# Decay in two waves, key norms in decay's bank, values masked from SBUF, another order on SyncE, and a last inverse on two engines

## The chip, the cores and the metric

The kernel runs on one core of a Trainium2 chip. The metric is the device time of one execution in microseconds (us). The median of the three runs of the kernel before is 1072.9 us.

## The reference

The input is x, 8 sequences of 512 tokens with 256 channels in float32. An attention-like layer with a recurrent state is followed by a mixture of eight experts. Cut to what matters here:

```python
xx = shift(x) - x;  lo = tanh((x + xx*maa_x) @ maa_w1.T) -> 4 x 32 -> @ maa_w2
xrg, xwa, xk, xv = x + xx*(lo + time_maa)
r, k, v = xrg @ Wr.T, xk @ Wk.T, xv @ Wv.T;   g = tanh(xrg @ gate_w1.T) @ gate_w2
w  = -softplus(-(time_decay + tanh(xwa @ decay_w1.T) @ decay_w2)) - 0.5
kk = k + tanh(xk @ kkk_w1.T) @ kkk_w2;  kk = kk / max(norm of each head(kk), 1e-12)
a, ma, mk = sigmoid(...)                       # three more low-rank products
k  = (k*ma + k*a*(1-ma)) * exp(w*mk);  b = -kk*a;  wt = exp(-exp(w))
for t in range(512):                           # state s: 16 x 16 for each head
    s = s*wt[t] + (s @ kk[t]) b[t]^T + v[t] k[t]^T;   y[t] = s @ r[t]
x1 = layernorm(x + ((groupnorm(y) + bonus*v) * g) @ Wo.T)
e  = argmax(x1 @ centroids.T)                  # one expert for each token
out = layernorm(x1 + ffn_e(layernorm(x1)))     # 256 -> 1024 -> 256, relu
```

## The kernel before

The 512 time steps are cut into 16 blocks of 32 steps (NBLK = 16, `last` = 15). Within a block the recurrence is solved with the inverse of a triangular 32x32 matrix for each of the 128 pairs of head and sequence, one pair in each partition. Every engine runs `body(n)` for n from -2 to 18, written out by hand. Body n computes the projections, decays, keys and scores of block n+1, turns keys and values of block n, solves and reads out block n-1, normalizes and projects block n-2, and routes block n-3. So several blocks are in flight, and each engine's order within a body is the order of the code. After the bodies, 39 blocks of 128 tokens go through the experts.

What sets the order around the change:

- **PSUM banks.** Six banks are handed from job to job. A job such as `z@1` (the decay's product in bank 1) may start when the job before it in that bank has been emptied, as the table `freed` says. PE waits for that with `wait_empty`.
- **TensorE (PE).** In `body`: `hidden`, `gates`, `square k`, `turn_keys`, then `decay_a_kk` and `ma_mk` (line 622), the router's `logit` and the projection `wo` of older blocks, `solve`, `norms`, the squares r and v, the read-outs, `scores` (line 662), `update`, and the next block's `low_1` and `low_2` (line 594). `fill` (line 576) is a helper that many of these use. All is float32, and each matmul leaves two records in the trace.
- **ScalarE (ACT).** `keep_k` (line 1085) copies k to SBUF; then come z plus its bias (line 1029, `halves`), its sigmoid, a, ma, |z|, the squares of kk, mk, a table load, the logarithm of sigma (line 1117), and much later `keep_v` and `mask_v`.
- **VectorE (DVE).** A body begins where `xm_stage` (lines 1389, 1392) of g=1 reads `low_2`. Then follow `normed`, the other xm stages, `keep_r`, `gated` (line 1536, which frees the bank of g for ma), `difference`, `mix_stage`, `sum_kk` (line 1420), `sum_decays`, `key_gain`, `add_tokens` (1546), `gain_keys`, `token_stats` (1552 to 1556), `key_exponent` (1412, which needs the logarithm), `keep_x` (1511), and the keys and removals down to `mask_keys` (1445), after which PE may start `scores`.
- **GpSimd (POOL).** It inverts one block per body with 60 small operations (lines 1911 and 1914), behind a memset of the diagonal (line 1904) that waits for the scores to come back from DRAM.
- **SyncE (SP).** One DMA queue: scores out (478), scores back as one matrix per partition (483), the inverse out (491), tokens for `add_tokens` (460), the inverse back by heads (502), tokens after the layer norm out (468), and the expert weights W2 (513), of which four are loaded in body 15 and four in body 16.

## Time and profile before

| | |
|---|---|
| runs | 1076.72, 1072.90, 1069.43 us; median 1072.9 |
| profiled execution | 1076.19 us, of which the span is 1074.1 us |
| mean granted TensorE clock | 0.951 |
| busy: PE / PE weight load | 980.1 us (91%) / 801.8 us (75%) |
| busy: DVE / ACT / POOL | 768.0 (71%) / 519.9 (48%) / 613.1 us (57%) |

Times in the rows are microseconds from the start of the span. The first 52 us are a start-up, the 15 repeated bodies run up to about 670 us, then comes a stretch of some 80 us with the last block and the routing, and from about 760 us the experts, in which PE is busy nearly all the time. "Busy" for PE counts modelled ends of pipelined matmuls.

### The profile page before, as it was taken

The page shows a single profiled execution, that of the slowest core. Times are in us where ns is not written, and L with a number is a line of the kernel's source. Part 1 is how long each engine was busy: PE and PEld are TensorE (multiplying, and loading weights), DVE is VectorE, ACT ScalarE, POOL GpSimd, SP SyncE. Part 2 cuts the span into 40 slices and gives each one's busy share as a digit, 9 for nine tenths or more (in the row PEclk, how much of TensorE's full clock was granted, in tenths as well). Part 3 has the DMA queues.
Part 4 walks back from the last instruction along what each step waited for, and adds up shares of the span by engine and source line. Part 5 has one row for each costly group of instructions (what it writes and reads, how often), then busy time and mean ns, then how long its engine had stood idle before and what let it go on. Part 6 is the DMA issues. An engine that isn't in the chain of part 4 may idle for free.

```text
span 1074.1 us, 42156 instructions
## 1 busy us (share of the span) xinstructions
PE 980.1 (91%) x16652; PEld 801.8 (75%) x16653; DVE 768.0 (71%) x1793; ACT 519.9 (48%) x1081; POOL 613.1 (57%) x1135
## 2 busy tenths in 40 slices
PE   8898989999999989999999998679899999999995
PEld 5676777777777767777777776557899898989894
DVE  5766788889879778887688885266476666666663
ACT  4474576677677576676476783221122121212120
POOL 1088786788886787785867876810133333333321
PEclk9997999999999999998799998689999999999998
DMA  5113225225324225224143133746545445544430
GB/s 121 40 21 81 71 33 110 65 51 111 77 47 101 70 44 111 72 42 107 17 101 87 28 91 85 206 115 232 217 163 176 161 174 162 176 158 170 158 119 4
DMA packets 208894, 112.14 MB, mean 104 GB/s; under 512 B 172508, under 2 KB 192224, under 8 KB 208352
## 3 DMA queue, kind: packets, MB, share of 16 engines
q1 hardware_dynamic: 202352, 100.92, 35.0%
q0 software_dynamic: 3744, 8.40, 2.3%
q8 instruction: 121, 1.98, 0.8%
q10 hardware_dynamic: 2640, 0.54, 0.3%
q14 instruction: 37, 0.30, 0.1%
HBM read 85.57 MB, written 26.08 MB: 104 GB/s over the span
## 4 chain that ended last, share of the span: by engine, by line
PE 61%; DVE 14%; issue 8%; POOL 6%; DMA 5%; ACT 4%; DVEq 1%; SPq 1%; ACTq 0%; POOLq 0%
PE bank L576 16%; PE bank L970 12%; PE bank L983 9%; PE bank L662 6%; PE ry L983 4%; PE bank L718 3%; POOL arena L1914 3%; POOL arena L1911 3%; DVE bank L1389 2%; PE ry L692 2%; PE bank L594 1%; PE bank L622 1%; PE bank L950 1%; PE ry L698 1%; PE bank L740 1%
## 5 line engine op out<-in xcount | busy, mean ns | idle before, releaser
L576 PE MATMUL bank<-arena 128*128 128x256 f32 (+2 forms) x992 | 280.9, 422 | 22.4 <-DVE arena L1434 9.5
L1914 POOL TENSOR_TENSOR arena<-arena 128x30 f32<-128x30 f32 (+14 forms) x480 | 261.6, 545 | 37.6
L1911 POOL TENSOR_TENSOR arena<-arena 128x30 f32<-128x30 f32 (+14 forms) x480 | 250.5, 522 | 36.4
L576 PEld LDWEIGHTS bank<-arena 128*128 128x128 f32 x992 | 178.5, 203 | 67.9 <-issue 31.5
L970 PEld LDWEIGHTS bank<-arena 128*128 128x128 f32 x1248 | 146.8, 194 | 5.8 <-issue 3.0
L970 PE MATMUL bank<-arena 128*128 128x128 f32 x1248 | 147.5, 277 | 3.1 <-DVE arena L1820 2.5
L1498 DVE TENSOR_TENSOR arena<-bank,arena 128x512 f32<-128x512 f32 x128 | 79.5, 684 | 53.1 <-PE bank L662 53.1
L1302 ACT ACTIVATE arena<-arena 128x1 f32<-128x1 f32 x39 | 11.5, 294 | 178.6 <-DVE arena L1774 178.6
L983 PE MATMUL bank<-arena 128*128 x416 | 96.4, 385 | 0.1
L1945 POOL COPY arena<-arena 128x1 int32 (+1 forms) x39 | 7.1, 183 | 146.4 <-DVE arena L1838 146.4
L983 PEld LDWEIGHTS bank<-arena 128*128 128x128 f32 x416 | 76.9, 190 | 14.5 <-issue 4.9
L662 PE MATMUL bank<-arena 32*128 32x64 f32 x2048 | 68.9, 276 | 10.6 <-issue 6.4
L1939 POOL DMA_INDIRECT arena<-scr_x,arena x39 | 41.2, 1056 | 62.4 <-DVE arena L1756 31.4
L662 PEld LDWEIGHTS bank<-arena 32*128 32x128 f32 x2048 | 64.0, 189 | 14.9 <-issue 13.4
L1389 DVE SCALAR_TENSOR_TENSOR bank<-bank,arena 128x256 f32<-128x256 f32 x128 | 56.1, 484 | 22.2 <-PE bank L594 22.2
L670 PE MATMUL bank<-arena 128*128 128x128 f32 x432 | 62.5, 279 | 4.2 <-DVE arena L1511 1.6
L670 PEld LDWEIGHTS bank<-arena 128*128 128x128 f32 x432 | 52.1, 144 | 18.8 <-issue 12.4
L1904 POOL MEMSET arena<- 128x32 f32 x16 | 2.5, 157 | 111.2 <-DMA arena<-scr_n 111.2
L718 PEld LDWEIGHTS bank<-arena 32*64 32x64 f32 x2048 | 40.1, 157 | 34.6 <-issue 29.6
L1820 DVE TENSOR_SCALAR arena<-bank,arena 128x128 f32<-128x128 f32 x156 | 43.9, 345 | 24.6 <-issue 19.9
L1947 POOL DMA_INDIRECT out_dram<-arena x39 | 39.8, 1021 | 34.9 <-DVE arena L1804 20.8
L718 PE MATMUL bank<-arena 32*64 32x32 f32 x2048 | 43.8, 239 | 15.1 <-DMA arena<-scr_u 13.9
(173 smaller groups left out, 1757.7 us busy)
## 6 DMA issues: line engine op xcount, KB each, us to landing
arena<-in_W SPq DMA_DIRECT2D x47, 1024.0 KB, 5.1
scr_n<-arena SPq DMA_DIRECT2D x64, 128.0 KB, 3.0
arena<-scr_n SPq DMA_DIRECT2D x16, 512.0 KB, 3.7
scr_u<-arena SPq DMA_DIRECT2D x16, 512.0 KB, 4.5
arena<-scr_u SPq DMA_DIRECT2D x62, 128.0 KB, 2.9
arena<-in_xTp SPq DMA_DIRECT2D x32, 132.0 KB, 4.0
arena<-in_x SPq DMA_DIRECT2D x64, 64.0 KB, 2.7
scr_x<-arena SPq DMA_DIRECT2D x64, 64.0 KB, 1.8
```

What stands on the lines that cost most here:

```text
L576: mm = pe.matmul(ring.tile(m, name)[0:rows, to], lhsT, rhs, start=(i == 0), stop=(i == len(terms) - 1))
L662: mm = pe.matmul(ring.tile(m, f"sc{f}{p}")[:, b * 2 * TB:(b + 1) * 2 * TB], bkm[r, f * B + b, :], aq[m % 2][r, f * B + b].rearrange("p x t ...
L670: mm = pe.transpose(ring.tile(m, name)[:, i * P:(i + 1) * P], src, ident)
L718: mm[bank] = pe.matmul(ring.tile(m, f"x{bank}")[x_rows_of(e), at:at + 32], Ux[m % 2][r, g % 4, g // 4, e].rearrange("p h t -> p (h t)"), R ...
L970: mm = pe.matmul(hidT_ps[t // 4][:, (t % 4) * P:(t % 4 + 1) * P], W1[s][:, k, t * P:(t + 1) * P], xnT[:, k, :], start=(k == 0), stop=(k == ...
L983: mm = pe.matmul(y_ps[s][:, 0:D], hidT[s][:, t, :], W2f[:, bass.ds(e * (FT * D) + t * D, D)], start=(t == 0), stop=(t == FT - 1))
L1389: xm_ok.inc(m, f"{g}{h}", STT(out=part, in0=part, scalar=prm(f"maa{g}", h), in1=dx[:, h], op0=ALU.add, op1=ALU.mult))
L1498: score.inc(m, name, TT(sc[m % 2][:, f, p].rearrange("p k e x t -> p (k e) (x t)"), ring.tile(m, name)[:, :].rearrange("p (b n) -> p b n", ...
L1820: relu_dve.inc(str(t), nc.vector.tensor_scalar(hidT[s][:, t], hidT_ps[1][:, (t - 4) * P:(t - 3) * P], b1f[:, bass.ds(e * FT + t, 1)], 0.0, ...
L1911: inv_ok.inc(f"m{s}", TT(t, U[:, 0:s, s:s + 1].broadcast_to(shape), U[:, s:s + 1, s + 1:TB].broadcast_to(shape), ALU.mult))
L1914: inv_ok.inc(f"a{s}", TT(U[:, 0:s, s + 1:TB], U[:, 0:s, s + 1:TB], t, ALU.add))
L1939: nc.gpsimd.indirect_dma_start(out=xg[:, s], out_offset=None, in_=x_rows, in_offset=bass.IndirectOffsetOnAxis(ap=index, axis=0), bounds_ch ...
```

## The change

The parts, as the code has them:

1. **Two waves.** The decay's product z was one matmul per half of the channels over all 128 rows (two slots), followed by two slots with a and kk side by side and two with ma and mk. Now z is cut into two products over 32 rows each. A first wave (two slots) runs the first z part, a and kk side by side in three row groups; a second wave runs the second z part, ma and mk. z is full only after the second.
2. **kk in k's bank.** The low-rank part of kk is added by PE into the bank where k stands, so it must wait until ACT has kept k. `sum_kk` on DVE is gone; ACT gets `keep_kk`, a copy of 128x512, and squares from PSUM. k moves ahead of the gates on PE.
3. **Banks.** `ss` goes to bank 1, `logit` to bank 0 ahead of `wo` in the same bank, `xa` to 5, `bk11` and `v0` to 0. The matmuls for `ss`, `yc` and `var` are two of 256 columns rather than one of 512.
4. **ACT order.** a before z; kk and its square, then the logits, before ma; `mask_v` reads SBUF and stands behind the second `keep_values`; `key_decay` and `growths` ahead of `keep_keys(1,1)`.
5. **DVE order.** `token_stats` moves behind `keep_decay`, `decay_reads` behind `bonus_terms`.
6. **SyncE.** Tokens are loaded behind the heads of the inverse; the inverse of block 14 is stored ahead of the scores' load of block 15; W2 is loaded in body 16 only.
7. **The last inverse.** POOL does the left 24 columns; DVE does the right 8 columns in bank 2, in three pieces among its other work of body 15.

```diff
@@ -356,7 +364,7 @@
         freed = {"lo1": [(low_act, "lo1")], "h": [(hid_act, "decay"), (hid_act, "copy"), (hid_act, "kkk")],
                  "z": [(comb, "scan")],
                  "a": [(proj, "a1")], "ma": [(comb, "k2")], "mk": [(comb, "e2")], "tg": [(proj, "tg")], "k": [(proj, "k")],
-                 "r": [(comb, "rk"), (comb, "q")], "v": [(proj, "v"), (proj, "vm1")], "kk": [(comb, "kk")], "ss": [(comb, "bm1")],
+                 "r": [(comb, "rk"), (comb, "q")], "v": [(proj, "v")], "kk": [(proj, "sq")], "ss": [(comb, "bm1")],
                  "rk": [(comb, "u")], "su": [(state_dve, "s")],
                  "yc": [(post_act, "c1"), (post_act, "s")], "var": [(post_dve, "w")], "g": [(post_dve, "g1")], "wo": [(tok, "z")],
                  "xT": [(late_act, "x1T")], "logit": [(late_act, "lg")]}
@@ -367,9 +375,9 @@
         freed["xa"] = [(chain_dve, "xae"), (chain_dve, "xao")]
         freed["xb"] = [(chain_act, "xb0"), (chain_act, "xb1"), (chain_dve, "xbo")]
         filled = [sem(f"filled{i}") for i in range(len(banks))]
-        ring = Ring(banks, [(0, "bk00@5"), (1, "h@2"), (-2, "g@4"), (1, "k@3"), (0, "bk01@2"), (1, "z@1 a@5 kk@3 ma@4 mk@2"),
-                            (-3, "logit@3"), (-2, "wo@0"), (1, "ss@0"), (-1, "xa@1 xb@3"), (1, "r@4"),
-                            (0, "bk11@5"), (1, "v@2"), (0, "bk10@5 v0@1 v1@3"),
+        ring = Ring(banks, [(0, "bk00@5"), (1, "h@2"), (1, "k@3"), (-2, "g@4"), (0, "bk01@2"), (1, "a@5 kk@3"),
+                            (1, "z@1 ma@4 mk@2"), (-3, "logit@0"), (-2, "wo@0"), (1, "ss@1"), (-1, "xa@5 xb@3"), (1, "r@4"),
+                            (0, "bk11@0"), (1, "v@2"), (0, "bk10@5 v0@0 v1@3"),
                             (1, "rk@4"), (-1, "su@0"), (1, "sc00@2 sc01@5 sc02@3 sc03@1 tg@4"), (2, "lo1@5"),
                             (1, "sc10@2 sc11@5 sc12@1 sc13@4"), (-1, "yc@3"), (2, "lo2_1@2 lo2_2@5 lo2_0@0 lo2_3@1"),
                             (-1, "var@4"), (-2, "xT@3")], filled, freed)
...
+                if m == last:
+                    store_inverse(last - 1)
                 sp.wait_ge(n_out, (m + 1) * 64)
                 if m >= 2:
                     sp.wait_ge(u_out, (m - 1) * 16)
                 sp.dma_start(Up[m % 2].rearrange("p r c -> p (r c)"),
                              nd.rearrange("g k f e (h s) t -> (g k f e h) (s t)", h=2)).then_inc(n_in, 16)
-
-            def inverse_to_heads(m):
-
-                inv_ok.wait(sp, m, "a1")
+                if m == last:
+                    heads_from_inverse(last - 1)
+
+            def store_inverse(m):
...
                 sp.dma_start(ud, Up[m % 2].rearrange("p r c -> p (r c)")).then_inc(u_out, 16)
-                if m == last:
-                    load_tokens(last)
-                elif m and m - 1 < last - 1:
-                    load_tokens(m - 1)
+
+            def heads_from_inverse(m):
+
...
                 for p in range(PAIRS if m < last else 2):
                     sp.dma_start(heads_of(m, p), u_rows[p]).then_inc(u_in, 16)
+                if m == last:
+                    load_tokens(last)
+                elif m and m - 1 < last - 1:
+                    load_tokens(m - 1)
...
             def body(n):
-                if has(n - 1):
-                    inverse_to_heads(n - 1)
+                if has(n - 1) and n != last:
+                    store_inverse(n - 1)
+                    heads_from_inverse(n - 1)
                 if has(n - 3) and n <= last:
                     store_x1(n - 3)
-                if n == last:
+                if n == last + 1:
+                    sp.wait_ge(u_in, NBLK * 64)
                     load_experts(slice(0, 4))
-                if n == last + 1:
                     load_experts(slice(4, E))
...
+                    ring.wait_empty(pe, m, name)
+                for h, to in both:
+                    mm_z = pe.matmul(ring.tile(m, "z")[:, to], w_out[0:32, 2, hs(h)], hid[0:32, :], start=(h == 0), stop=False,
+                                     skip_group_check=True)
+                    mm_a = pe.matmul(ring.tile(m, "a")[:, to], w_out[64:96, 0, hs(h)], hid[64:96, :], start=True, stop=True)
+                    mm_kk = pe.matmul(ring.tile(m, "kk")[:, to], w_out[96:128, 0, hs(h)], kkh[96:128, :], start=False, stop=True,
+                                      skip_group_check=True)
+                mm_z.then_inc(half_decay, 1)
+                ring.fill(m, "a", mm_a)
+                ring.fill(m, "kk", mm_kk)
+
+            def decay_ma_mk(m):
+                pe.wait_ge(half_decay, m + 1)
+                for name in ("ma", "mk"):
+                    ring.wait_empty(pe, m, name)
+                for h, to in both:
+                    mm_z = pe.matmul(ring.tile(m, "z")[:, to], w_out[32:64, 2, hs(h)], hid[32:64, :], start=False, stop=True,
+                                     skip_group_check=True)
+                    mm_ma = pe.matmul(ring.tile(m, "ma")[:, to], w_out[64:96, 1, hs(h)], hid[64:96, :], start=True, stop=True)
+                    mm_mk = pe.matmul(ring.tile(m, "mk")[:, to], w_out[96:128, 1, hs(h)], hid[96:128, :], start=True, stop=True)
+                ring.fill(m, "z", mm_z)
+                ring.fill(m, "ma", mm_ma)
+                ring.fill(m, "mk", mm_mk)
 
             def square(m, name, w, x):
                 weights(m)
                 xm_ok.wait(pe, m, f"x{x}")
-                fill(m, name, [(to, [(w_sq[:, w, k, hs(h)], xm[x][:, k]) for k in range(HALF)]) for h, to in both])
+                fill(m, name, [(to, [(w_sq[:, w, k, hs(h)], xm[x][:, k]) for k in range(HALF)]) for h, to in both],
+                     started_once=(name == "k"))
 
...
+                proj.inc(m, "sq", A(flat(nrm), bank(m, "kk"), ACT.Square))
+
+            def keep_kk(m):
+                if m:
+                    comb.wait(act, m - 1, "kkn")
+                ring.wait_full(act, m, "kk")
+                proj.inc(m, "kk", A(flat(kk), bank(m, "kk"), ACT.Copy))
...
+                proj.wait(act, m, "v")
                 for h in range(2):
-                    proj.inc(m, f"vm{h}", A(vm[:, :, h], bank(m, "v").rearrange("p (g t) -> p g t", t=TB), ACT.Copy,
-                                            scale=odd_even[:, h:h + 1]))
+                    proj.inc(m, f"vm{h}", A(vm[:, :, h], tt(vt), ACT.Copy, scale=odd_even[:, h:h + 1]))
...
+            def keep_coefs(m):
+                act.wait_ge(n_in, (m + 1) * 16)
+                last_inv.wait(act, 0, "diag")
+                comb.wait(act, m, "e2")
+                A(coefs, Up[m % 2][:, 0:CUT, 0:CUT], ACT.Copy).then_inc(coefs_kept, 1)
...
                 if has(n + 1):
+                    keep_a(n + 1)
                     keep_z(n + 1)
                     sigma_of_z(n + 1)
-                    keep_a(n + 1)
+                    keep_kk(n + 1)
+                    square_kk(n + 1)
+                if has(n - 3):
+                    keep_logits(n - 3)
+                if has(n + 1):
                     keep_ma(n + 1)
                     abs_of_z(n + 1)
-                if has(n - 3):
-                    keep_logits(n - 3)
                 if n == last + 1:
                     second_inverse_to_heads(last)
                 if has(n + 1):
-                    square_kk(n + 1)
                     sigma_of_abs(n + 1)
                     keep_mk(n + 1)
...
+                if has(n + 1):
+                    key_decay(n + 1)
+                    growths(n + 1)
                 if has(n) and n < last:
                     keep_keys(n, 1, 1)
...
                 if has(n + 1):
                     keep_v(n + 1)
-                    mask_v(n + 1)
                 if has(n):
                     keep_values(n, 1)
+                if has(n + 1):
+                    mask_v(n + 1)
...
+            def start_right(m):
+                dve.wait_ge(n_in, (m + 1) * 16)
+                last_inv.wait(dve, 0, "diag")
+                last_inv_dve.inc("start", nc.vector.tensor_copy(right, Up[m % 2][:, :, CUT:TB]))
+                dve.wait_ge(coefs_kept, 1)
+                proj.wait(dve, m, "iW0", "iW1")
+
+            def invert_right(m, steps):
+                U = Up[m % 2]
+                for s in steps:
+                    last_inv_dve.wait(dve, 0, "start" if s == TB - 2 else f"a{s + 1}")
+                    c = max(s + 1, CUT) - CUT
+                    n = TB - CUT - c
+                    shape = [P, s, n]
+                    t = flat(L)[:, 0:s * n].rearrange("p (r c) -> p r c", r=s)
+                    column = U[:, 0:s, s:s + 1] if s >= CUT else coefs[:, 0:s, s:s + 1]
+                    last_inv_dve.inc(f"m{s}", TT(t, right[:, s:s + 1, c:].broadcast_to(shape), column.broadcast_to(shape), ALU.mult))
+                    last_inv_dve.wait(dve, 0, f"m{s}")
+                    last_inv_dve.inc(f"a{s}", TT(right[:, 0:s, c:], right[:, 0:s, c:], t, ALU.add))
+
+            def keep_right(m):
+                last_inv_dve.wait(dve, 0, "a1")
+                last_inv_dve.inc("kept", nc.vector.tensor_copy(Up[m % 2][:, :, CUT:TB], right))
...
-                if has(n - 2):
+                if has(n - 2) and not has(n + 1):
                     token_stats(n - 2)
                 if has(n + 1):
                     key_exponent(n + 1)
+                if n == last:
+                    start_right(last)
+                    invert_right(last, range(TB - 2, 23, -1))
                 if has(n - 1):
                     keep_x(n - 1, "a", 0)
                     keep_x(n - 1, "a", 1)
                     keep_x(n - 1, "b", 1)
+                if n == last:
+                    invert_right(last, range(23, 12, -1))
                 if has(n + 1):
                     normed_kk(n + 1)
-                    decay_reads(n + 1)
                     decay_kk(n + 1)
                     removal(n + 1)
                     decay_keys(n + 1)
                     bonus_terms(n + 1)
+                    decay_reads(n + 1)
                 if has(n + 1):
                     mask_removal(n + 1)
                     mask_keys(n + 1)
                     bonus_values(n + 1)
                     keep_decay(n + 1)
+                if has(n - 2) and has(n + 1):
...
+            def invert_left(m):
+
+                pool.wait_ge(n_in, (m + 1) * 16)
+                U = Up[m % 2]
+                inv_ok.wait(pool, m - 1, "a1")
+                last_inv.inc("diag", nc.gpsimd.memset(U.rearrange("p r c -> p (r c)")[:, 0:TB * TB:TB + 1], 1.0))
+                pool.wait_ge(coefs_kept, 1)
+                for s in range(CUT - 2, 0, -1):
+                    n = CUT - 1 - s
+                    shape = [P, s, n]
+                    t = Ut[:, 0:s * n].rearrange("p (r c) -> p r c", r=s)
+                    if s < CUT - 2:
+                        last_inv.wait(pool, 0, f"a{s + 1}")
+                    last_inv.inc(f"m{s}", TT(t, U[:, 0:s, s:s + 1].broadcast_to(shape), U[:, s:s + 1, s + 1:CUT].broadcast_to(shape),
+                                             ALU.mult))
+                    last_inv.wait(pool, 0, f"m{s}")
+                    last_inv.inc(f"a{s}", TT(U[:, 0:s, s + 1:CUT], U[:, 0:s, s + 1:CUT], t, ALU.add))
+
+            for m in range(NBLK - 1):
                 invert(m)
+            invert_left(last)
```

PE, in the middle of the program, from `hidden` of one block to the `wo` of an older one (bank0 to bank5 are the six banks; L610/L631 is `hidden`, L670/L698 `turn_keys`). Before:

```order
L610 MATMUL bank2<-arena 32x256 x8
L576 MATMUL bank4<-arena 128x256 x2
L576 MATMUL bank3<-arena 128x256 x4
L670 MATMUL bank2<-arena 128x128 x4
L622 MATMUL bank1<-arena 128x256 x2
L622 MATMUL bank5<-arena 128x256
L622 MATMUL bank3<-arena 128x256
...
L576 MATMUL bank3<-arena 128x8 x4
L576 MATMUL bank0<-arena 128x256 x4
```

and now:

```order
L631 MATMUL bank2<-arena 32x256 x8
L596 MATMUL bank3<-arena 128x256 x4
L596 MATMUL bank4<-arena 128x256 x2
L698 MATMUL bank2<-arena 128x128 x4
L640 MATMUL bank1<-arena 128x256
L642 MATMUL bank5<-arena 128x256
L643 MATMUL bank3<-arena 128x256
...
L654 MATMUL bank1<-arena 128x256
L656 MATMUL bank4<-arena 128x256
...
L596 MATMUL bank0<-arena 128x8 x4
L596 MATMUL bank0<-arena 128x256 x4
```

z (bank1) was complete two matmuls after `turn_keys`; now its last matmul stands in the second wave, beside ma's in bank4, and logit (128x8) and wo share bank0.

ACT at the same place, from `keep_k` to the logarithm. Before:

```order
L1085 ACTIVATE arena<-bank3 128x512
L1150 ACTIVATE arena<-bank2 128x512
L1029 ACTIVATE arena<-bank1,arena 128x256 x2
L1058 ACTIVATE bank1<-arena 128x512
L1029 ACTIVATE arena<-bank5,arena 128x256 x2
L1029 ACTIVATE bank4<-bank4,arena 128x256 x2
L1064 ACTIVATE arena<-arena 128x512
L1212 ACTIVATE arena<-bank3 128x16
L1097 ACTIVATE arena<-arena 128x512
L1068 ACTIVATE arena<-arena 128x512
L1029 ACTIVATE bank2<-bank2,arena 128x256 x2
L1035 ACT_TABLE_LOAD
```

and now:

```order
L1182 ACTIVATE arena<-bank2 128x512
L1057 ACTIVATE arena<-bank5,arena 128x256 x2
L1057 ACTIVATE arena<-bank1,arena 128x256 x2
L1086 ACTIVATE bank1<-arena 128x512
L1130 ACTIVATE arena<-bank3 128x512
L1124 ACTIVATE arena<-bank3 128x512
L1244 ACTIVATE arena<-bank0 128x16
L1057 ACTIVATE bank4<-bank4,arena 128x256 x2
L1092 ACTIVATE arena<-arena 128x512
L1096 ACTIVATE arena<-arena 128x512
L1057 ACTIVATE bank2<-bank2,arena 128x256 x2
L1063 ACT_TABLE_LOAD
```

a (bank5) went ahead of z (bank1), the copy of kk from bank3 (L1130) is new, and the logits (128x16) are read two operations later.

SyncE's queue in one body, from the scores' load. Before:

```order
L483 DMA arena<-scr_n 128x1024 [waits u_out,n_out]
L491 DMA scr_u<-arena 128x1024 [waits u_in,inv_ok]
L460 DMA arena<-in_x 32x2x256 [waits x1_out,filled3]
L460 DMA arena<-in_x 32x2x256 x3
L502 DMA arena<-scr_u 32x32x32 [waits filled3,u_out]
L502 DMA arena<-scr_u 32x32x32 x3
```

and now:

```order
L493 DMA arena<-scr_n 128x1024 [waits u_out,n_out]
L507 DMA scr_u<-arena 128x1024 [waits u_in,inv_ok]
L517 DMA arena<-scr_u 32x32x32 [waits filled3,u_out]
L517 DMA arena<-scr_u 32x32x32 x3
L468 DMA arena<-in_x 32x2x256 [waits x1_out,filled3]
L468 DMA arena<-in_x 32x2x256 x3
```

The four token loads (in_x) went from ahead of the four loads of heads to behind them.

## Rows read from the trace of the kernel before

**Rows 1.** Busy time by stretch: PE, PEld, DVE, ACT, POOL, granted clock, DMA share, GB/s.

```profile
257.20:298.30 41.10, 38.08 (x921) 29.62 (x917) 35.64 (x64) 29.94 (x59) 35.48 (x68) 1.00 0.43 90
380.40:421.40 41.00, 37.43 (x905) 29.04 (x904) 32.87 (x61) 26.82 (x50) 33.04 (x63) 0.96 0.34 75
```

**Rows 2.** Timeline, DVE, one body: start, us, operation, [idle before, releaser].

```profile
326.85 0.88 DVE L1389 SCALAR_TENSOR_TENSOR bank<-bank,arena 128x256 f32<-128x256 f32 x2 [0.70 <-PE bank L594]
...
334.95 0.83 DVE L1536 SCALAR_TENSOR_TENSOR arena<-arena,bank 128x256 f32<-128x256 f32 x2
...
337.41 0.68 DVE L1420 TENSOR_TENSOR arena<-bank,arena 128x512 f32<-128x512 f32 x1
...
341.20 0.69 DVE L1546 TENSOR_TENSOR arena<-bank,arena 128x512 f32<-128x512 f32 x1 [0.67 <-PE bank L576]
...
342.40 0.75 DVE L1552 BATCH_NORM_STATS2 arena<-arena 128x6 f32<-128x256 f32 x2
...
343.35 0.93 DVE L1412 SCALAR_TENSOR_TENSOR arena<-arena 128x512 f32<-128x512 f32 x1
...
352.13 1.75 DVE L1445 TENSOR_TENSOR arena<-arena 128x512 f32<-128x512 f32 x2
```

**Rows 3.** Timeline, ACT, the same body.

```profile
334.41 0.60 ACT L1085 ACTIVATE arena<-bank 128x512 f32<-128x512 f32 x1 [0.95 <-PE bank L576]
...
335.72 0.84 ACT L1029 ACTIVATE arena<-bank,arena 128x256 f32<-128x256 f32 x2 [0.22 <-PE bank L622]
...
337.12 0.82 ACT L1029 ACTIVATE arena<-bank,arena 128x256 f32<-128x256 f32 x2
...
342.53 0.63 ACT L1117 ACTIVATE arena<-arena 128x512 f32<-128x512 f32 x1
```

**Rows 4.** Timeline, PE, the same body.

```profile
325.59 1.15 PE L594 MATMUL bank<-arena 32*128 32x256 f32 x16
...
334.59 2.96 PE L622 MATMUL bank<-arena 128*128 128x256 f32 x20
338.23 2.86 PE L576 MATMUL bank<-arena 128*128 128x8 f32 x16 [0.69 <-DVE arena L1420]
...
342.08 1.13 PE L576 MATMUL bank<-arena 128*128 128x512 f32 x2
...
346.47 1.89 PE L576 MATMUL bank<-arena 128*128 128x256 f32 x8
```

**Rows 5.** Timeline, DVE, another body: its first operation and its key_exponent.

```profile
450.69 0.88 DVE L1389 SCALAR_TENSOR_TENSOR bank<-bank,arena 128x256 f32<-128x256 f32 x2 [2.00 <-PE bank L594]
...
468.76 1.05 DVE L1412 SCALAR_TENSOR_TENSOR arena<-arena 128x512 f32<-128x512 f32 x1
```

**Rows 6.** Timeline, SP's queue, the body of rows 2; then issues, 300 to 400 us, median landing.

```profile
331.50 2.64 SPq L460 DMA_DIRECT2D arena<-in_x  x4
335.18 2.67 SPq L502 DMA_DIRECT2D arena<-scr_u  x4
...
arena<-in_x SPq DMA_DIRECT2D x8, 64.0 KB, 2.9
```

**Rows 7.** One line, L1904: durations in ns, first and last start in us.

```profile
L1904 POOL MEMSET arena<- x16: 154/158/162, 52.2 to 668.0; 128x32 f32 x16
```

**Rows 8.** The chain that ended last, around the last solve.

```profile
702.91 2.76 DMA scr_u<-arena
...
710.15 1.97 PE bank L718 x64
```

**Rows 9.** Timeline, DVE, 655 to 765 us: last tokens' wait, and small operations.

```profile
670.96 0.69 DVE L1546 TENSOR_TENSOR arena<-bank,arena 128x512 f32<-128x512 f32 x1 [6.11 <-DMA arena<-in_x]
...
703.67 0.39 DVE L1579 TENSOR_TENSOR arena<-arena 128x224 f32<-128x224 f32 x1
...
738.73 0.77 DVE L1710 TENSOR_TENSOR arena<-bank,arena 128x8 f32<-128x8 f32 x4 [0.72 <-PE bank L930]
```

**Rows 10.** Timeline, POOL, an inverse operation of 130 elements.

```profile
656.71 0.44 POOL L1914 TENSOR_TENSOR arena<-arena 128x130 f32<-128x130 f32 x1
```

## What the change should do to the time

> **What bounds the kernel now.** I read the table of stretches first. In the repeated bodies PE is busy 37.4 to 38.1 us of 41, DVE 33 to 36, POOL 33 to 35, ACT 27 to 30 [rows 1], so no engine is the bound by its share alone. The bodies have a mean length of (668.0 - 52.2) / 15 = 41.05 us [rows 7]. Which wait ends last is read from one body, engine by engine.
>
> DVE starts the body at 326.85, when PE's `low_2` is there, and works without a gap to 337.41, idles 0.67 us at `add_tokens`, and goes on to the end of `mask_keys` at 353.88 [rows 2]. Only then may PE start `scores`. So from the start of a body to `mask_keys`, 27.0 us, DVE is the chain; from there to the next body's start PE is. PE waits for DVE in the first part too: 0.69 us for `sum_kk`, which empties bank 3 for the router's logits [rows 4].
>
> One point inside DVE's stretch is tied to ACT. `key_exponent` starts at 343.35 [rows 2] and needs the logarithm that ACT finishes at 342.53 + 0.63 = 343.16 [rows 3]. In the timeline ACT works back to back from 335.72, the start of z, to that logarithm: 7.44 us. So DVE may be made shorter ahead of `key_exponent` as one likes: it then waits for ACT.
>
> **The bodies, term by term.**
>
> PE's saving. The group of L622 is six slots of 256 columns in 2.96 us [rows 4], 0.49 each. In L594 eight matmuls in four row groups take 1.15 us for two slots [rows 4], so three side by side should cost one slot. Six slots become four: 0.98 us less. One matmul of 512 columns takes 1.13 us, four of 256 take 1.89 [rows 4], so two of 256 take 0.95: 0.18 less, or by the start of the next group 0.12. I take 0.15, three times. PE has 1.4 us less to do in each body.
>
> DVE's saving. `sum_kk` 0.68 us goes, and `token_stats`, 343.35 - 342.40 = 0.95 us, moves behind `keep_decay`, where DVE waits for `scores` anyway [rows 2]. 1.6 us less ahead of `key_exponent`. `decay_reads` only changes places ahead of `mask_keys`; it is worth nothing there.
>
> What z now waits for. Wave 2 writes ma in bank 4, which `gated` empties at 334.95 + 0.83 = 335.78 [rows 2]. Two slots later, at 335.8 + 1.0 = 336.8, z is full. Before, z was full after the first two slots, 334.59 + 0.98 = 335.57 [rows 4], and ACT started on it at 335.72 [rows 3]. ACT's z therefore starts at about 336.95, 1.2 us later. It does a (0.82 us [rows 3]) in the meantime and still idles 0.35. Then z to the logarithm takes 7.44 - 0.82 (a is done) + 0.60 (the copy `keep_kk`, priced as the copy `keep_k` [rows 3]) = 7.2 us, so the logarithm is ready at 344.2 and `key_exponent` starts at about 344.3 instead of 343.35: 0.95 us later. DVE would have been there at 341.7. All of DVE's 1.6 us is idle time, and what lies behind `key_exponent` is unchanged up to `mask_keys`.
>
> In PE's order the projection `wo` now shares bank 0 with the logits, which ACT reads at about 339.6. PE idles near 1.8 us before it; its `wo` is full near 341.7, where `add_tokens` could start 0.5 us after its place of now. That is hidden by the wait for ACT.
>
> So a body like this one becomes 0.95 us longer up to `mask_keys`. From there to the next start only the halved `yc` counts: 0.15 less. Together +0.8.
>
> Not every body is like this. From a body's start to `key_exponent` it is 16.5 us here [rows 2] and 18.07 in another [rows 5]; the same two operations give 16.1 to 16.8 in eight of the 13 full bodies and 17.9 to 18.6 in five, where PE's slower `wo` held DVE up. In those five the ACT chain (17.45) is shorter than what there is, and PE's saving gives back 0.2 to 0.4. The mean over the 13 is (8 x 0.85 - 5 x 0.3) / 13 = +0.4, less 0.15 for `yc`: about +0.3 us for each body, **+4 us** in all. Bounds: -1.35 for each body if ACT is not in the way (rival A), +1 if every body is like the first.
>
> By the Trainium skill, page "TensorEngine Tiling (Array Packing)", section "PSUM Bottleneck", tiling speeds up TensorE but not the emptying of PSUM, and the copies may become the bottleneck. By PE's slots alone the body would be 1.4 us shorter; by the page's rule, which here is the ACT chain above, it is longer.
>
> **Masks, values, banks.** `mask_v` out of SBUF costs the same on ACT and moves behind `keep_values`. Nothing waits for it before the next body. I put nothing on it. `ss` in two halves falls in PE's slack.
>
> **SyncE.** Token loads are issued at 331.50 and the heads at 335.18, when the stored inverse has landed [rows 6]. The heads are held by that landing, not by the token loads, so they gain nothing. The tokens now follow: the last is issued near 337.85 + 2.0 and lands 2.9 later [rows 6], at 342.8; `add_tokens` and `gain_keys` are then over at 344.1, just ahead of the new `key_exponent`. Zero in this body, with no room left.
>
> **The last inverse.** POOL starts the last one at 668.0 [rows 7] and its result is stored at 702.91 [rows 8]: 34.9 us. Nothing of the next blocks covers it; `solve` starts 7.24 us behind the store [rows 8]. POOL's left part has 44 operations of at most 132 elements, 0.44 us each [rows 10] and some 0.06 between them: under 22 us, over before 691. DVE's right part decides. An operation of 8 elements follows the one before it in 0.20 us (four in 0.77), one of 224 takes 0.39 [rows 9]; that is 0.19 + 0.9 ns for each element. The 60 operations have 2 x 2936 elements: 11.4 + 5.3 = 16.7 us, two copies 0.8, some gaps: 19. It starts behind `add_tokens` and its statistics for block 13, which waited for tokens until 670.96 [rows 9]. In the new queue the inverse of block 14 is stored about 5.7 us earlier, but the tokens stand behind its heads: they land near 672, the statistics end at 674, and DVE's part starts there. `keep_x` 2.0, `next_state` 1.4 and `tokens` 0.9 lie between its pieces. 674 + 19 + 4.3 = 697.5, against 702.9: **-5 us**. The rest behind it runs as before, W2's load included: it is 8 MB from body 16 on, needed only some 60 us later. Bounds: -7 (tokens land early), 0 (strided operands on DVE cost 1.3 times as much).
>
> **Sum.** 1076.2 (the profiled execution, 1074.1 of span and 2.1 around it) + 4 - 5 = 1075. That execution is 3.3 us above the median of the three runs, so against the median: **1072 us**, no change that can be measured. About 1% is what a measurement of this kernel can tell from none.
>
> **The rivals.**
>
> A, faster: PE sets the period after all, and ACT keeps up, because its operations overlap more than I allow or because `gated` comes earlier. Then each of 14 bodies gives back PE's 1.35 us: -19, with the inverse -24: 1049 us. For it: PE is busy over 91% of a body [rows 1]. Against it: ACT has no gap between z and the logarithm. Chance 0.34.
>
> B, slower: the granted clock. One stretch ran at 1.00, another at 0.96 [rows 1]; 0.04 of 41 us is 1.6 us of PE time given up, at 1.2 instead of 2.4 GHz for some 3.3 us. In the change PE has less to do and new idle places, 1.8 us ahead of `wo` and about 1 us ahead of `scores`. If every body loses those 1.6 us where about half do now, that is +0.8 x 14 = 11, with all bodies at +0.8 for ACT another 11, less 5: 1090 us. It decides once the mean granted clock of the bodies falls under about 0.95. Chance 0.16.
>
> The Trainium skill, "TensorE: Matmul & The Clock Gate", section "What's actually happening", says that the slow clock is the default and activity releases it. The difference between the two stretches fits that; by it, the less PE has to do, the more often B.
>
> C, slower: tokens too late. In bodies where the stored inverse lands 1 to 2 us later than in [rows 6], `add_tokens` holds DVE for as long. +0.7 x 14 = 10: 1082 us. For it: there is no room left even in the body shown. Chance 0.08.
>
> The forecast has 0.42. The range leaves out a tenth on each side: 1048 to 1088; the forecast's own is 1064 to 1081. Faster by over 1%: 0.34. Within 1%: 0.42. Slower: 0.24.
>
> **What would show it.** Right: DVE waits 1 us or more before `key_exponent` and names ACT; its start is 17.3 to 17.6 us behind the body's start; the mean length of a body, from one diagonal memset to the next, stays 41 to 41.6 us; the last inverse takes 29 to 30 us from its memset to its store. Wrong: bodies under 40 us with PE busy near 37 (A); a mean clock under 0.94 (B); `add_tokens` waiting for `in_x` in most bodies (C); DVE's operations for the right part at 0.4 us each, which would leave the last inverse no shorter.

## The result, and the profile after

| | before | changed |
|---|---|---|
| median | 1071.2 us (4 runs) | 1117.4 us (4 runs) |
| ratio to before | | 1.0425, 95% interval 1.0364 to 1.0487 |
| span of the profiled execution | 1074.1 us | 1117.0 us |
| mean granted clock | 0.951 | 0.922 |
| first diagonal memset | 52.2 us | 54.7 us |
| last diagonal memset | 668.0 us | 708.6 us |
| from one to the next | 41.05 us | 43.60 us |
| last memset to the first gather of the experts | 82.4 us | 82.7 us |
| the experts to the end | 323.6 us | 325.6 us |

Medians are over all executions of a kernel; the ratios leave out the few that ran in a slower state. The change made the kernel 4.25% slower, 46 us. The forecast was 1072 us, at the top 1088. Of the 42.9 us between the two spans, 2.5 are there before the first memset, 15 x 2.54 = 38.1 in the bodies, 0.3 between the last memset and the experts, and 2.0 in the experts. The bodies are the case. The profiled execution of the kernel before took 1076.19 us, 5 above its median, that of the changed kernel 1118.81, 1.4 above, so 2.54 us for each body is rather too little than too much.

The memset that opens each inverse answers to [rows 7]. In the changed kernel the last one has a line of its own. The trace, by source line: durations in ns, first and last start in us.

```profile
L1974 POOL MEMSET arena<- x15: 154/157/162, 54.7 to 664.0; 128x32 f32 x15
L1991 POOL MEMSET arena<- x1: 156/156/156, 708.6 to 708.6; 128x32 f32 x1
```

The page of the changed kernel: busy time, the granted clock in 40 slices, and the costliest group of instructions.

```profile
span 1117.0 us, 42510 instructions
PE 1001.3 (90%) x16812; PEld 833.6 (75%) x16813; DVE 776.4 (70%) x1839; ACT 536.0 (48%) x1098; POOL 597.5 (53%) x1119
PEclk9997998899989999788799997888999999999998
L596 PE MATMUL bank<-arena 128*128 128x256 f32 (+1 forms) x1088 | 310.6, 430 | 41.0 <-ACT arena L1244 22.5
```

What is new in the last line is what ends TensorE's idle time: the same line before reads 22.4 us idle and names VectorE. L1244 is ScalarE's copy of the router's logits, and TensorE idles 22.5 us in all for it. The waits of TensorE and VectorE in the bodies (230 to 650 us; us in total, times, longest) say how often:

```profile
PE bank L596 <- ACT arena L1244: 17.8, 10, 1.8
...
DVE arena L1443 <- ACT bank L1086: 13.3, 10, 1.6
DVE arena L1549 <- PE bank L746: 12.6, 7, 3.1
...
DVE arena L1608 <- DMA arena<-in_x: 2.0, 1, 2.0
```

1.8 us in each of ten bodies, ahead of `wo`. What comes behind it is to be seen in the timeline of TensorE in one of them (line 596 is `fill`, 746 `solve`, 698 `turn`; each matmul leaves two records, so x8 are four matmuls):

```profile
317.23 1.06 PE L596 MATMUL bank<-arena 128*128 128x8 f32 x8
320.07 2.77 PE L596 MATMUL bank<-arena 128*128 128x256 f32 x8 [1.78 <-ACT arena L1244]
322.76 1.93 PE L746 MATMUL bank<-arena 32*64 32x32 f32 x64
324.63 2.08 PE L596 MATMUL bank<-arena 128*128 128x256 f32 x4
326.63 1.93 PE L746 MATMUL bank<-arena 32*64 32x32 f32 x64
328.49 3.37 PE L596 MATMUL bank<-arena 128*128 128x256 f32 x8
331.70 0.60 PE L698 MATMUL bank<-arena 128*128 128x128 f32 x4
332.14 1.89 PE L596 MATMUL bank<-arena 128*128 128x256 f32 x8
```

Four matmuls of 256 columns take 3.37 us at 328.49, and the next four, at 332.14, take 1.89 as in [rows 4]. The rows of the stretches (columns as in [rows 1]) give the granted clock:

```profile
320.10:321.00 0.90, 0.90 (x4) 0.80 (x5) 0.33 (x2) 0.90 (x3) 0.74 (x3) 1.00 0.64 184
321.10:331.30 10.20, 10.20 (x144) 7.88 (x143) 6.27 (x10) 7.71 (x14) 9.10 (x15) 0.50 0.27 50
332.00:333.00 1.00, 1.00 (x7) 0.91 (x6) 0.90 (x3) 0.60 (x1) 0.85 (x2) 1.00 0.00 0
```

The clock is at full speed in the first microsecond of `wo`, then at half for 10.2 us in which TensorE is busy without a gap. From `wo` to the end of the square r it is 331.86 - 320.07 = 11.8 us; in a kernel below, where nothing runs slowly, 7.1. On VectorE, in the same body, it arrives as the wait of `keep_x` (line 1549) for the solve:

```profile
307.13 0.88 DVE L1432 SCALAR_TENSOR_TENSOR bank<-bank,arena 128x256 f32<-128x256 f32 x2 [0.69 <-PE bank L615]
...
318.95 1.22 DVE L1443 TENSOR_TENSOR_SCAN arena<-arena,bank 128x512 f32<-128x512 f32 x1 [1.19 <-ACT bank L1086]
320.74 0.69 DVE L1449 SCALAR_TENSOR_TENSOR arena<-bank,arena 128x512 f32<-128x512 f32 x1 [0.57 <-ACT bank L1057]
...
324.51 0.69 DVE L1455 SCALAR_TENSOR_TENSOR arena<-arena 128x512 f32<-128x512 f32 x1 [0.28 <-ACT arena L1149]
...
328.61 2.01 DVE L1549 TENSOR_TENSOR arena<-bank,arena 64x512 f32<-64x512 f32 x3 [2.69 <-PE bank L746]
...
335.95 1.75 DVE L1483 TENSOR_TENSOR arena<-arena 128x512 f32<-128x512 f32 x2
```

`key_exponent` (1455) starts 17.38 us behind the body's start, as forecast. But `keep_x` (1549) then waits 2.69 us for a solve at half speed, and from `key_exponent` to `mask_keys` (1483) it is 11.44 us. In [rows 2] that is 8.78, and `keep_x` does not wait.

### The profile page after: what moved, and what is told of

The parts are those of the page before. It is cut to its first block, busy times and chain, and to the rows that moved or that the text cites. A ratio compares the mean times of both kernels' runs of the same rounds, so it can differ in the third digit from the quotient of the medians.

```text
span 1117.0 us, 42510 instructions
## 1 busy us (share of the span) xinstructions
PE 1001.3 (90%) x16812; PEld 833.6 (75%) x16813; DVE 776.4 (70%) x1839; ACT 536.0 (48%) x1098; POOL 597.5 (53%) x1119
## 4 chain that ended last, share of the span: by engine, by line
PE 65%; DVE 15%; issue 8%; ACT 6%; DVEq 2%; DMA 2%; SPq 1%; POOL 0%; ACTq 0%; POOLq 0%
PE bank L596 20%; PE bank L1011 9%; PE bank L998 6%; PE bank L690 6%; PE bank L746 3%; PE bank L698 3%; PE ry L720 2%; PE ry L726 2%; PE bank L615 2%; PE bank L768 1%; PE bank L654 1%; PE bank L631 1%; DVEq L1830 1%; PE ry L1011 1%; PE ry L821 1%
## 5 line engine op out<-in xcount | busy, mean ns | idle before, releaser
L596 PE MATMUL bank<-arena 128*128 128x256 f32 (+1 forms) x1088 | 310.6, 430 | 41.0 <-ACT arena L1244 22.5
L596 PEld LDWEIGHTS bank<-arena 128*128 128x128 f32 x1088 | 217.5, 220 | 95.3 <-issue 50.3
L1984 POOL TENSOR_TENSOR arena<-arena 128x30 f32<-128x30 f32 (+14 forms) x450 | 244.0, 542 | 35.3
L1981 POOL TENSOR_TENSOR arena<-arena 128x30 f32<-128x30 f32 (+14 forms) x450 | 236.5, 526 | 34.1
L998 PEld LDWEIGHTS bank<-arena 128*128 128x128 f32 x1248 | 146.8, 194 | 6.1 <-issue 3.3
L1011 PEld LDWEIGHTS bank<-arena 128*128 128x128 f32 x416 | 76.9, 190 | 14.5 <-issue 4.9
L698 PE MATMUL bank<-arena 128*128 128x128 f32 x432 | 63.1, 279 | 9.2 <-DVE arena L1549 6.3
L698 PEld LDWEIGHTS bank<-arena 128*128 128x128 f32 x432 | 51.7, 143 | 19.4 <-issue 10.6
L746 PEld LDWEIGHTS bank<-arena 32*64 32x64 f32 x2048 | 43.8, 171 | 20.8 <-issue 14.2
L2036 POOL DMA_INDIRECT out_dram<-arena x39 | 39.8, 1021 | 34.9 <-DVE arena L1874 20.8
L1360 ACT ACTIVATE arena<-bank,arena 128x128 f32<-128x128 f32 x156 | 44.6, 369 | 26.4 <-PE bank L998 26.4
```

The costliest lines, as they stand in the source:

```text
L596: mm = pe.matmul(ring.tile(m, name)[0:rows, to], lhsT, rhs, start=(i == 0 and not (started_once and j)), stop=(i == len(terms) - 1), skip_ ...
L698: mm = pe.transpose(ring.tile(m, name)[:, i * P:(i + 1) * P], src, ident)
L746: mm[bank] = pe.matmul(ring.tile(m, f"x{bank}")[x_rows_of(e), at:at + 32], Ux[m % 2][r, g % 4, g // 4, e].rearrange("p h t -> p (h t)"), R ...
L998: mm = pe.matmul(hidT_ps[t // 4][:, (t % 4) * P:(t % 4 + 1) * P], W1[s][:, k, t * P:(t + 1) * P], xnT[:, k, :], start=(k == 0), stop=(k == ...
L1011: mm = pe.matmul(y_ps[s][:, 0:D], hidT[s][:, t, :], W2f[:, bass.ds(e * (FT * D) + t * D, D)], start=(t == 0), stop=(t == FT - 1))
L1360: relu_act.inc(str(t), A(hidT[s][:, t], hidT_ps[0][:, t * P:(t + 1) * P], ACT.Relu, bias=b1f[:, bass.ds(e * FT + t, 1)]))
```

## The experiments

All kernels were timed beside runs of the kernel before on the same chip; each ratio is to those, with its 95% interval. "Body" is the mean from one diagonal memset to the next in one profiled execution, worked out as in the table above; two executions of a kernel can differ in it by 0.5 us and more (those of the kernel before that the ratios use took 1063 to 1080 us, which is 1.1 us for each body), so small differences are read from the ratios. "Clock" is the granted clock from 93 to 639 us of that execution. "Idle" is TensorE's wait for the logits ahead of `wo`, in one body; the kernel before waits 0.7 us elsewhere, for `sum_kk` [rows 4]. An unread matmul has 256 columns and takes some 0.5 us.

| kernel | idle | clock | body | ratio |
|---|---|---|---|---|
| before | none | 0.96 | 41.05 | 1 |
| changed | 1.8 | 0.89 | 43.60 | 1.0425 [1.0364, 1.0487] |
| changed, one unread matmul | 1.3 | 0.95 | 42.04 | 1.0255 [1.0147, 1.0363] |
| changed, logits before kk | 0.8 | 0.96 | 41.35 | 1.0217 [1.0119, 1.0316] |
| changed, three unread matmuls | 0.4 | 0.97 | 41.26 | 1.0142 [1.0066, 1.0218] |
| changed, early logits | none | 0.97 | 41.99 | 1.0242 [1.0150, 1.0335] |
| changed, z first | 0.6 | 0.95 | 41.41 | 1.0045 [0.9991, 1.0100] |
| before, shared bank | 0.9 | 0.92 | 42.02 | 1.0184 [1.0100, 1.0267] |
| before, shared bank, two unread matmuls | none | 0.97 | 40.51 | 1.0027 [0.9993, 1.0060] |
| before, waves | none | 0.93 | 41.80 | 1.0135 [1.0044, 1.0227] |

### The wait itself, or the clock behind it

Three matmuls that nobody reads fill most of the wait; the wait for ScalarE's copy stays.

```diff
+                if has(n - 3) and n < last:
+                    ring.wait_empty(pe, n - 1, "xa")
+                    keep_busy(3, banks[5])
                 if has(n - 2):
                     project_out(n - 2)
```

> The changed kernel with three matmuls of 256 columns, whose result nobody reads, put on TensorE between the logits and `wo` in bodies 3 to 14 (bank 5, which is free there). They take about 1.4 of the 1.8 us that TensorE idles; the wait for ScalarE's copy of the logits stays where it is, `wo` starts when it did. It tells the wait itself from the clock that falls behind it. If the clock is what costs (theory T in its clock form): `wo` takes 1.9 us instead of 2.8, the solve 1.13 us instead of 1.93, the bodies come down by 1.5 to 2 us, about 1090 to 1095 us. If the wait itself costs: 1115 to 1118 us, with bodies of 43.5 us at a higher clock.

Measured: 1086.3 us, under the 1090 to 1095 expected. The timeline of TensorE at the same place of a body (line 821 is `keep_busy`; each matmul leaves two records):

```profile
348.80 1.06 PE L596 MATMUL bank<-arena 128*128 128x8 f32 x8
349.72 1.54 PE L821 MATMUL bank<-arena 128*128 128x256 f32 x6
351.65 1.97 PE L596 MATMUL bank<-arena 128*128 128x256 f32 x8 [0.39 <-ACT arena L1247]
353.54 1.13 PE L746 MATMUL bank<-arena 32*64 32x32 f32 x64
354.60 1.13 PE L596 MATMUL bank<-arena 128*128 128x256 f32 x4
355.67 1.13 PE L746 MATMUL bank<-arena 32*64 32x32 f32 x64
356.73 1.99 PE L596 MATMUL bank<-arena 128*128 128x256 f32 x8
```

`wo` starts 2.85 us behind the logits' start, as in the changed kernel (320.07 - 317.23 = 2.84). Nothing came sooner, TensorE only had more to do, and every group runs at full speed. That took away 2.8 of the 4.25 percent. For these 2.8, the clock is what costs, not the wait. The row of the stretch, for the changed kernel and then for this one (columns as in [rows 1]):

```profile
93.00:639.00 546.00, 494.52 (x11231) 397.54 (x11224) 411.39 (x734) 364.38 (x674) 401.84 (x763) 0.89 0.32 69
```

```profile
93.00:639.00 546.00, 499.55 (x12047) 400.72 (x12039) 438.54 (x778) 382.29 (x706) 421.63 (x807) 0.97 0.34 73
```

0.89 x 43.60 = 38.8 and 0.97 x 41.26 = 40.0: counted roughly at full clock, the body of the changed kernel is no longer than that with the filler, which holds 1.5 us of unread work.

The mean clock of whole executions says the same. It is 0.925 for the changed kernel and 0.965 with the three matmuls (four executions each), 31 us for 0.040, or 8 us for each 0.01. The kernel before has its own measure: over 55 executions, from 1063 us at 0.966 to 1080 us at 0.945, its time falls by some 7 us for each 0.01.

What is left, 1.4%, is not the clock, which is here above that of the kernel before (0.954). VectorE waits for ScalarE 32.5 us in the ten bodies, against 1.0 in the kernel before: 15.1 at the scan for the sigmoid of z, 6.5 at `key_gain` for ma, and 10.9 at `key_exponent` for the logarithm. This is the sign that the forecast had asked for, and it shows once the solve is in time (the wait, then the same operation in the body above):

```profile
DVE arena L1458 <- ACT arena L1152: 10.9, 11, 1.1
```

```profile
356.09 0.82 DVE L1458 SCALAR_TENSOR_TENSOR arena<-arena 128x512 f32<-128x512 f32 x1 [1.08 <-ACT arena L1152]
```

From that body's start at 338.07 to `key_exponent` it is 18.02 us, and from there to `mask_keys` 9.30.

### How the cost goes with the length of the idle place

One unread matmul in place of three:

```diff
-                    keep_busy(3, banks[5])
+                    keep_busy(1, banks[5])
```

> The changed kernel with one unread matmul of 256 columns (0.47 us) ahead of `wo` instead of three; `wo` starts when it did, and 1.3 us of idle time are left. If the cost goes with the idle time: 1.025 to 1.035 of the kernel before, clock near 0.935. If it needs the whole wait filled: 1.038 to 1.045.

Measured: 1095.2 us. And without a filler, ScalarE's copy of the logits two operations sooner:

```diff
                     sigma_of_z(n + 1)
+                if has(n - 3):
+                    keep_logits(n - 3)
+                if has(n + 1):
                     keep_kk(n + 1)
                     square_kk(n + 1)
-                if has(n - 3):
-                    keep_logits(n - 3)
```

> The changed kernel with one line moved on ScalarE: the copy of the logits stands ahead of the copy of kk and its squares instead of behind them. Waves, banks and TensorE's order are those of the changed kernel, and no filler is added. ScalarE's sigmoid of z ends at 318.85 in the body that begins at 307.13, so the logits are out near 319.0 instead of 319.9, and TensorE waits 0.8 us ahead of `wo` instead of 1.8. If the cost goes with the idle time: between the changed kernel and the one with three unread matmuls, nearer to the latter, 1.020 to 1.030 of the kernel before, clock 0.94 to 0.95. If any such wait brings the slow clock: 1.035 to 1.045.

Measured: 1092.0 us. The waits of TensorE from 230 to 650 us, with one unread matmul, and with the logits before kk:

```profile
PE bank L596 <- ACT arena L1247: 13.7, 11, 1.3
```

```profile
PE bank L596 <- ACT arena L1244: 8.1, 10, 0.8
```

1.8, 1.3, 0.8 and 0.4 us of idle time go with ratios of 1.043, 1.026, 1.022 and 1.014. Most of the gain comes with the first half microsecond that is filled; the three later ones lie within each other's intervals, and their order alone is not shown. The mean clock of whole executions goes the same way: 0.925, 0.947, 0.954 and 0.965.

The idle time that counts is not TensorE's total. Summed over all its waits from 230 to 650 us it is 38.0 us in the changed kernel and 29.7 with three unread matmuls, but 51.4 us with the early logits below, where the clock is 0.97, and 26.8 us in the kernel before with the shared bank, next, where it is 0.92, against 29.5 without it. Where the idle time lies matters as well; by what rule, these runs do not show.

### The shared bank in the old kernel

One entry of the bank table puts the logits of the kernel before into bank 0, ahead of `wo`.

```diff
-                            (-3, "logit@3"), (-2, "wo@0"), (1, "ss@0"), (-1, "xa@1 xb@3"), (1, "r@4"),
+                            (-3, "logit@0"), (-2, "wo@0"), (1, "ss@0"), (-1, "xa@1 xb@3"), (1, "r@4"),
```

> The kernel before with one entry of the bank table changed: the logits go to bank 0, ahead of `wo` in the same bank, as in the changed kernel, and no longer to bank 3. Nothing else moves. TensorE no longer waits 0.7 us for `sum_kk` ahead of the logits, but waits for ScalarE's copy of the logits ahead of `wo`, here at about 339.5, so some 1.3 to 1.8 us. Theory T: this alone brings most of the loss, bodies of 42.5 to 43.5 us, 1095 to 1110 us against 1072. Rivals W and D: the wait stays hidden behind ScalarE's chain, 1070 to 1078 us.

Measured: 1091.0 us, below the 1095 to 1110 expected of theory T and above the 1070 to 1078 of its rivals: the wait was 0.9 us, not 1.3 to 1.8. Then the same with two unread matmuls in bank 3 behind the logits:

```diff
+                if has(n - 3) and n < last:
+                    ring.wait_empty(pe, n - 1, "xb")
+                    keep_busy(2, banks[3])
                 if has(n - 2):
                     project_out(n - 2)
```

> The kernel before with the logits in bank 0 ahead of `wo` (the run of the shared bank, 1.018 of the kernel before, mean clock 0.939), and two unread matmuls of 256 columns in bank 3 between the logits and `wo`, about 0.95 us, where TensorE waited 0.9 us in each body. Clock theory: the mean clock comes back to 0.95 or more and the ratio to 1.000 to 1.006, 1074 to 1080 us. If the wait itself costs: 1.015 to 1.02 still.

Measured: 1074.4 us. The rows of the stretch, without and with them:

```profile
93.00:639.00 546.00, 507.29 (x11783) 393.88 (x11785) 429.66 (x772) 362.56 (x680) 416.84 (x789) 0.92 0.32 70
```

```profile
93.00:639.00 546.00, 507.53 (x12097) 397.48 (x12093) 446.88 (x805) 377.13 (x709) 432.65 (x817) 0.97 0.34 72
```

So it is not something peculiar to the changed kernel. 0.9 us of idle time ahead of `wo`, in place of 0.5 us (4.9 us in ten bodies) ahead of the logits, costs the old one 1.8%, and work without a use in its place gives nearly all of it back. The intervals of the two do not meet.

### The waves

The changed kernel with z first and alone, as before (six slots, z over all 128 rows; ScalarE does z, its sigmoid, then a):

```diff
+                from_hidden(m, [[("z", 2, slice(0, P), hid)]])
+                from_hidden(m, [[("a", 0, slice(64, 96), hid), ("kk", 0, slice(96, 128), kkh)]])
...
+                from_hidden(m, [[("ma", 1, slice(64, 96), hid), ("mk", 1, slice(96, 128), hid)]])
...
-                    keep_a(n + 1)
                     keep_z(n + 1)
                     sigma_of_z(n + 1)
+                    keep_a(n + 1)
```

> The changed kernel with the two waves undone: z is computed first and alone as one product of 64 hidden rows, as before, then a with kk, then ma with mk (six slots instead of four), and ScalarE starts with z and does a behind its sigmoid, as before. Banks, the shared bank 0, the order of all else stay as changed. Theory T: z is ready about 1 us earlier, the wait ahead of `wo` stays 1 us or more and so does the slow clock; 1105 to 1120 us. Rival W: this is the whole cost, 1072 to 1085 us.

Measured: 1079.4 us, 1.0045. My expectation was wrong by 26 us or more, and rival W's held in its number. It is no proof of W, for the edit moved two things at once: TensorE reaches `wo` later and ScalarE the logits sooner, so the idle place shrank to 0.6 us and the clock rose to 0.95. But the clock cannot be all of it. Over whole executions it is 0.947, the same as in the kernel with one unread matmul, and that one stands at 1.0255; the two intervals do not meet. At the same clock, z first is 2.1% faster, some 22 us or 1.5 us for each body. So the waves with their order on ScalarE cost nearly as much as the clock does (2.8%; together more than the whole 4.25%, so the two overlap or another part of the change gives something back). That the late z is the cause of those 2.1% is argued from the waits on ScalarE, not shown by itself: z first together with the unread matmuls was not run. The kernel before with the waves alone parts them, since there nothing new stands ahead of `wo` (`decay_a_kk` and `decay_ma_mk` are those of the change, but kk starts its bank by itself):

```diff
+                    decay_ma_mk(n + 1)
-                    ma_mk(n + 1)
...
+                    keep_a(n + 1)
                     keep_z(n + 1)
                     sigma_of_z(n + 1)
-                    keep_a(n + 1)
```

> The kernel before with only the waves: z in two halves of 32 hidden rows beside a with kk and ma with mk, four slots instead of six, and a ahead of z on ScalarE. `sum_kk` stays on VectorE, the logits stay in bank 3, so that nothing new stands ahead of `wo`. Theory W' (z reaches ScalarE 1 us later and VectorE waits for it, the clock stays as it was): bodies of 41.3 to 42 us, 1076 to 1088 us against 1072. Rival A of the prediction (TensorE's saved slots shorten the body): bodies under 40.5 us, 1050 to 1066 us. Theory T: the clock does not fall by more than 0.01 against the kernel before.

Measured: 1086.9 us, 1.0135. Its waits from 230 to 650 us:

```profile
DVE arena L1406 <- ACT bank L1064: 13.4, 11, 2.0
...
DVE arena L1418 <- ACT arena L1123: 2.4, 8, 0.3
```

VectorE waits 1.2 us in each body for the sigmoid of z, where the kernel before does not wait at all. The body became 0.75 us longer. Rival A, that TensorE's saved slots shorten the body, is refuted: there are two slots less and the kernel is slower. The clock fell too, to 0.93 in the bodies of this execution; over the whole of four executions it is 0.949 against 0.956, within the 0.01 that I had expected. By the 7 us for each 0.01 of the kernel before, this is an estimated 5 of the 14.5 us; the rest would be the late z. With three unread matmuls in the changed kernel 1.4% is left, a similar amount, but that kernel differs in other parts too.

The logits of the changed kernel computed ahead of the waves, and copied out ahead of a:

```diff
+                if has(n - 3):
+                    router(n - 3)
                 if has(n + 1):
                     decay_a_kk(n + 1)
...
+                if has(n - 3):
+                    keep_logits(n - 3)
                 if has(n + 1):
                     keep_a(n + 1)
```

> The changed kernel, with one job moved: the router's logits are computed on TensorE ahead of wave 1 instead of behind wave 2, and ScalarE copies them out ahead of a instead of behind the squares of kk. The bank stays 0, the projection `wo` still follows in it, but the logits are out long before `wo` is due, so the idle 1.8 us of each body ahead of `wo` should be gone (the waves start some 0.6 us later for it). Theory T (the shared bank makes TensorE idle 1.8 us, it then runs at half clock, and the solve with all behind it comes late): bodies near 41.5 us from one diagonal memset to the next instead of 43.6, 15 x 2 us less, about 1085 to 1090 us instead of 1117. Rival W (the two waves hand z to ScalarE late, and that is what costs): bodies get no shorter, rather 0.5 us longer, 1115 to 1125 us. Rival D (VectorE's and SyncE's new order costs): 1110 to 1117 us.

Measured: 1099.0 us, a miss by 10. The wait ahead of `wo` is gone and the clock is 0.97. But the waves start later. Against the kernel with three unread matmuls, at the same clock of 0.97 in the bodies, a body is 0.73 us longer, and one wait of VectorE (230 to 650 us) is 0.77 us longer in each body, 2.28 where it was 1.51:

```profile
DVE arena L1443 <- ACT bank L1086: 22.8, 10, 3.9
```

Here a body is lengthened at full clock by the chain from z over ScalarE to VectorE. It is the chain on which the forecast rests.

### Reads of the decay, and a better order on ScalarE

The changed kernel with three unread matmuls and `decay_reads` back in its old place:

```diff
                     normed_kk(n + 1)
+                    decay_reads(n + 1)
                     decay_kk(n + 1)
```

> The changed kernel with the three unread matmuls ahead of `wo`, and `decay_reads` back in its old place, ahead of `decay_kk`. In the run with the filler alone TensorE waited 1.4 us in each body for `decay_reads` ahead of `bonus`, whose bank it empties (in the kernel before 0.7 us, for `bonus_terms`). If that wait is part of what is left of the loss: 0.2 to 0.5 us less for each body, 1078 to 1083 us instead of 1086. If it is covered by the wait for `mask_keys` behind it, as the prediction says: 1085 to 1088 us.

Measured: 1084.6 us, 1.0100 [1.0039, 1.0162]. TensorE's wait ahead of `bonus` fell from 14.3 us over ten bodies (for `decay_reads`) to 9.3 (for `bonus_terms`), and the time by nothing that can be told from none. The move of `decay_reads` costs nothing measurable.

On top of z first, ma sooner on ScalarE, and the tokens of block 13 early as in a run below:

```diff
                     keep_ma(n + 1)
+                    keep_kk(n + 1)
+                    square_kk(n + 1)
```

> Meant to beat both. The changed kernel with z first (as in the run with z first), ScalarE's order z, sigmoid, a, logits, ma, kk, squares, |z| instead of z, sigmoid, a, kk, squares, logits, ma, |z|, and the tokens of block 13 early. In the run with z first VectorE waited 1.2 us in each body for ScalarE's ma and TensorE 0.6 us for the logits; both should go, and the squares of kk come 1 us later, still ahead of the solve that needs their bank. Expected: bodies near 40.6 us instead of 41.4, 12 us less from them and 3 from the tokens, 1060 to 1066 us against 1079 of z first and 1077 of the kernel before in those comparisons. Rival: VectorE's gain turns into a wait for the logarithm, bodies stay at 41.2 us, 1072 to 1077 us.

Measured: 1081.0 us, 1.0085 [1.0053, 1.0116], slower than the kernel before. The rival's mechanism came true, its 1072 to 1077 us did not: bodies are 41.5 us. VectorE's wait for the logarithm (line 1452 here, for ScalarE's line 1145), 3.2 us over four bodies with z first, became:

```profile
DVE arena L1452 <- ACT arena L1145: 12.2, 10, 2.1
```

### The last inverse

The kernel before with the split inverse alone, and W2 behind the last heads:

```diff
+                if n == last:
+                    start_right(last)
+                    invert_right(last, range(TB - 2, 23, -1))
...
-            for m in range(NBLK):
+            for m in range(NBLK - 1):
                 invert(m)
+            invert_left(last)
```

> The kernel before with only the last inverse changed: its right eight columns on VectorE, its left 24 on GpSimd, the copy of the coefficients on ScalarE, and the W2 load behind the last heads, since the coefficients lie where W2 goes. Bodies, banks and SyncE's other order are those of before. The prediction: from the last diagonal memset to the store 28 to 30 us instead of 34.9, the solve 5 us sooner, 1067 us against 1072. Rival P (the time behind the store is bound by TensorE and by the tokens, not by the inverse): the store comes 5 to 6 us sooner, but the solve and the first gather of the experts by 0 to 3 us only, 1070 to 1074 us.

Measured: 1070.2 us, 0.9963 [0.9913, 1.0013]: a gain that cannot be told from none. In us, from the last memset to:

| kernel | store | solve | first gather |
|---|---|---|---|
| before | 34.9 | 42.1 | 82.4 |
| changed | 28.3 | 39.8 | 82.7 |
| before, split inverse | 28.7 | 38.7 | 79.2 |
| changed, three unread matmuls | 30.1 | 40.4 | 81.2 |
| the same, tokens early | 26.0 | 36.3 | 77.2 |

Each row is one execution. In these, in the old kernel 3.4 are left of 6.2 at the solve and 3.2 at the first gather; in the changed one 2.3 of 6.6 at the solve and nothing at the gather. Over all kernels only the first column is firm: the store comes after 26.0 to 30.7 us in the twelve with a split inverse and after 34.7 to 34.9 in the five without. The gather comes after 77.2 to 85.3 us in the twelve (mean 81.3) and after 82.2 to 83.6 in the five (mean 82.9), so of some 5 us at the store about 1.6 arrive at the experts, and what a single row has there is mostly scatter. The changed kernel's timeline of TensorE behind the store at 736.90 (lines 828 and 829 rank the known tokens, 780 reads out):

```profile
738.31 3.55 PE L596 MATMUL bank<-arena 128*128 128x256 f32 x12 [2.38 <-DVE arena L1592]
742.23 3.75 PE L596 MATMUL bank<-arena 128*128 128x256 f32 x8 [0.36 <-ACT arena L1244]
745.78 0.95 PE L828 MATMUL bank<-arena 128*128 128x224 f32 x2
...
747.27 1.27 PE L821 MATMUL bank<-arena 128*128 128x256 f32 x4
748.47 2.35 PE L746 MATMUL bank<-arena 32*64 32x32 f32 x128
753.03 1.19 PE L780 MATMUL ry<-arena 128*32 128x32 f32 x109 [2.20 <-DVE arena L1549]
757.03 0.54 PE L780 MATMUL ry<-arena 128*32 128x32 f32 x19 [2.82 <-issue]
```

The solve does not wait for the heads any more. TensorE works up to it, at half clock (3.75 us for four matmuls, x8), on what VectorE could give it only once its part of the inverse was through. Behind the solve it waits 2.20 us for `keep_x`, and then, among the read-outs, 2.82 us for nothing that the profile shows.

Tokens of block 13 ahead of the stored inverse of block 14, in the changed kernel with three unread matmuls:

```diff
                 if m == last:
+                    load_tokens(last - 2)
                     store_inverse(last - 1)
```

> The changed kernel with the three unread matmuls ahead of `wo` (as in the run with the filler alone) and with the tokens of block 13 loaded ahead of the stored inverse of block 14 instead of behind its heads. In the run with the filler alone `add_tokens` of block 13 held VectorE for 5.9 us for them, and VectorE's part of the last inverse stands behind it. If that wait sets the end of the last inverse: it is stored some 5 us sooner, from the last memset to the store 23 to 24 us, and 3 to 5 us come off the filler's 1086 us: 1081 to 1083 us. If TensorE sets the solve (theory P): the store comes sooner and the solve does not, 1085 to 1087 us.

Measured: 1086.9 us, as without. In the table the store, the solve and the gather come 4 us sooner, the store later than the 23 to 24 us expected. That the early tokens bring these 4 us is not shown: three other kernels with them store after 29.3 to 30.7 us, and the one with one unread matmul and late tokens has its solve after 36.3 and its gather after 78.5. The wait that goes is this one in the changed kernel (VectorE's timeline; its part of the inverse starts at 714.23, right behind):

```profile
712.55 0.69 DVE L1608 TENSOR_TENSOR arena<-bank,arena 128x512 f32<-128x512 f32 x1 [5.54 <-DMA arena<-in_x]
```

Both edits put into the kernel before, without and with one unread matmul ahead of the logits (the second with this besides):

```diff
+                if has(n - 3) and n < last:
+                    ring.wait_empty(pe, n - 2, "wo")
+                    keep_busy(1, banks[0])
                 if has(n - 3):
                     router(n - 3)
```

> Meant to beat both: the kernel before with the split last inverse, and with the tokens of block 13 loaded ahead of the stored inverse of block 14. In the run with the split alone the split brought 3 us from the last memset to the first gather; in the changed kernel with the filler the early tokens brought another 4. Expected 3 to 5 us less than the split alone, 1064 to 1068 us, 0.990 to 0.995 of the kernel before. Rival P (TensorE sets the end of the tail): 1070 us, as the split alone.

> The same as the split with early tokens, with one unread matmul of 256 columns (about 0.5 us) in bank 0 ahead of the logits, where TensorE of the kernel before waits 0.7 us for `sum_kk`. Clock theory: the mean clock rises from 0.955 to above 0.965, 0.2 to 0.4 us less for each body, 3 to 6 us less than without it. Otherwise the same time within 2 us, or up to 2 us more where the matmul comes late.

Measured: 1075.1 us, 0.9976 [0.9934, 1.0018], and 1071.8 us, 0.9983 [0.9953, 1.0014]. Neither beats the kernel before by more than can be measured, and the one is no faster than the other. The clock of the old kernel is at 0.96 in its bodies already, and over whole executions it rose only from 0.958 to 0.962 with the unread matmul.

### The tokens behind the heads

The kernel before with SyncE's other order alone:

```diff
-                if m == last:
-                    load_tokens(last)
-                elif m and m - 1 < last - 1:
-                    load_tokens(m - 1)
                 sp.wait_ge(u_out, (m + 1) * 16)
...
                     sp.dma_start(heads_of(m, p), u_rows[p]).then_inc(u_in, 16)
+                if m == last:
+                    load_tokens(last)
+                elif m and m - 1 < last - 1:
+                    load_tokens(m - 1)
```

> The kernel before with SyncE's token loads behind the heads instead of ahead of them, nothing else. The prediction puts this at zero, with no room left: 0.998 to 1.003 of the kernel before, `add_tokens` waiting for them in none or a few of the bodies. Rival C: 1.005 to 1.012, with that wait in most bodies.

Measured: 1081.9 us, 1.0102 [0.9976, 1.0229]: not settled. Its trace has `add_tokens` waiting for the tokens in three bodies between 230 and 650 us, 5.7 us in all, and 9.65 us in the one of the last inverse; the changed kernel in one body, 2.0 us. It may cost the old kernel some microseconds. In the changed one it hardly shows, perhaps because VectorE comes to that place later.

## Why the prediction was wrong

- **What bounds the body, and the chain over ScalarE: right.** VectorE waits for ScalarE, `key_exponent` starts 17.38 us behind the body's start (forecast 17.45, to be seen at 17.3 to 17.6). One sign failed: the wait stands earlier, at the scan (1.19 us) and at `key_gain` (0.57), and only 0.28 us of it at `key_exponent`. It stands where forecast only in kernels whose stall ahead of `wo` is filled or gone (1.0 us in each body with three unread matmuls).
- **TensorE's saving: too large.** Two waves took 2.3 us from the first matmul at 314.97 to the logits, 0.7 less than the 2.96 of [rows 4] and not 0.98. It changed nothing.
- **The wait ahead of `wo`: the step that failed.** I wrote that TensorE idles near 1.8 us there and that this "is hidden by the wait for ACT". The length was right, 1.78 us. The hiding was not. `wo` itself was not the trouble: `add_tokens` waited 0.78 us. What I left out of the sum is what comes next on the engine that idled. It ran at a mean clock of 0.89 instead of 0.96 in the bodies, so the two solves and the norms between them ended late, and `keep_x`, which stands behind `key_exponent` where I had called everything unchanged, waited 2.69 us. Cover for one consumer (`add_tokens`) is no cover for the rest of the engine's queue.
- **Rival B: the right mechanism, too cheap and too unlikely.** I priced it at 1.6 us in half of the bodies, 0.8 us for each, because I took the loss of one slow stretch of the old kernel as its size. With the fillers as measure it is 43.60 - 41.26 = 2.34 us for each body (2.1 by the medians, 31 us in 15 bodies), near three times that; with that, the forecast's 1072 would have become 1107 or 1103. The bound that I gave ("under about 0.95") was passed by far. The sentence of the Trainium skill that I had set beside it, page "TensorE: Matmul & The Clock Gate", section "What's actually happening", that activity releases the slow clock, is what the fillers show: work that nobody reads took the clock from 0.89 to 0.97.
- **The late z: the second term that failed, by its size.** With the clock restored the changed kernel is still 1.4% slower than before, 15 us, where the sum had +4 for the bodies and -5 for the inverse. The waves alone measure 1.35% [0.44, 2.27], so the +0.3 us for a body was too small; 0.75 was measured, where the body I had worked through said +0.8. At the same clock z first is 2.1% faster. The chain over ScalarE was the right mechanism; the discount for the five slower bodies made it too small, for with the clock restored VectorE waits for ScalarE in every one of the ten bodies.
- **The last inverse: right at the store, wrong at the end.** 28.3 us against 29 to 30 forecast, and VectorE's part took the 19 us of the sum: 22.6 us from 714.23 to the end of the copy back, less 4.0 of other work between its pieces, is 18.6. "The rest behind it runs as before" was wrong: in the changed kernel the store to the solve took 11.6 us instead of 7.2.
- **Rival A: refuted** by the waves alone. **Rival C:** one wait of 2.0 us in the changed kernel's bodies, as the forecast had it.
- **Open:** the 2 us in the experts, which most kernels made from the changed one show in part (1.3 to 1.8), one of them not at all, and the 2.5 us before the first memset, of which the waves alone show 1.2.

## What to carry to other kernels

When an edit puts a new wait on TensorE, do not ask only who needs the matmul behind it, but what the whole engine does behind it at half speed and who waits for that; where other work bounds the kernel, a stall of 1 to 2 us in each round can cost more than its own length (here 1.4 us that were filled brought 2.1). The quick test is to fill the idle place with matmuls into a free bank: if the time falls though nothing starts sooner, it is the clock. Do not stop there: compare kernels at the same mean clock, for a second cost can hide behind the first, as the late z did here. And a bank that two jobs share one behind the other ties TensorE to the engine that empties it, so the copy between them belongs first in that engine's queue.

## What the runs showed of the hardware

- After a stall of 1.78 us TensorE worked for 1 us at full clock and then for 10.2 us at half (granted clock 0.50 from 321.1 to 331.3), busy all that time: four matmuls of 256 columns in 3.37 us, 64 records of the solve in 1.93. Then it ran at full speed again (1.89 us for four). These are its two levels, 1.2 and 2.4 GHz. In the body with 0.39 us left of the stall the clock stayed at 1.00 and the same groups took 1.99 and 1.13 us.
- In this series the mean granted clock of the bodies fell with the idle time ahead of `wo`: 0.97 with 0.4 us idle, 0.96 with 0.8, 0.95 with 1.3, 0.89 with 1.8. It did not go with TensorE's total idle time: 0.97 with 51.4 us of waits, 0.92 with 26.8 (in 420 us).
- Unread matmuls, 1.5 us of them in each of 12 bodies, made a kernel 31 us faster (1117.4 to 1086.3 us, medians of different comparisons), some 8 us for each 0.01 of the mean clock of the execution.
- A wave of two slots, three matmuls side by side, took 1.19 and 1.07 us from its first matmul to that of the next group (314.97 to 316.16 to 317.23, with a semaphore between the two), where z alone over all rows took 0.96 in the kernel before (334.59 to 335.55).
